# Spreading an attention tile's loads and store over its eight head units

## The chip, the cores and the metric

The kernel runs on one core of one Trainium2 chip. The metric is the device time in microseconds (us) of one execution, as the median of several runs. The trace is one profiled execution of the same program.

## The reference

Four graph layers follow each other on x (2708 nodes, 512 features) and a dense 0/1 adjacency `adj` (2708 x 2708), each wrapped as `x = layernorm(x + layer(x, adj))`. The change touches the first, an eight-head attention whose mask is the adjacency with ones on its diagonal:

```python
adj = jnp.maximum(adjacency_matrix, jnp.eye(n))
keys, queries, values = (jnp.einsum('nj,hjk->hnk', node_matrix, W) for W in (Wks, Wqs, Wvs))
atts = jnp.einsum('hqk,hmk->hqm', queries, keys) / key_dim ** 0.5
atts = atts - 1e+16 * (1.0 - adj)[None, :, :]
atts = jax.nn.softmax(atts, axis=-1)
return jnp.einsum('hqm,hmk,hko->qo', atts, values, Wo)
```

The other three layers (a matrix product with the adjacency, an edge attention, a normalised product) are not touched.

## The kernel before

All matrix work is fp16 with each operand split in a high and a low half, so a product is three matmuls; sums are fp32. `project` makes keys (`kk`) and values (`vv`), which stay in SBUF, and queries, which go to DRAM as `q_rows`. Then `attention` runs over T = 22 tiles of 128 query rows, and in each tile over H = 8 heads. One (tile, head) pair is a unit, numbered i = 8t + h. Every engine runs the same loop of steps (`all_steps`): in step h of tile t an engine works on units that lie 0 to 4 steps back, given by `on(back)` and `unit(m, u, h, back)`. Tiles are written in pairs, t = 2m + u, and tiles 3 to 20 are a hardware loop of two tiles per turn (`pairs`).

The life of a unit:

- PE (`scores`, L641) makes the scores in three pieces of keys, 1024, 768 and 916 wide, in two PSUM slots.
- DVE (`mask`, L766) adds the mask tile `adj[:, u, ...]`, which holds 0 where there is an edge and a huge negative number where there is none, and writes `sc`; then `largest` (L776) makes the row maximum.
- One step later ACT takes the exponential of the pieces (L719) and rounds piece 0 to fp16 (`part_high`, L735); POOL (`low`, L603, and the copy L615) makes the rest of the halves of pieces 0 and 1.
- In the same step SP turns pieces 0 and 1 by DMA (L578), four `dma_start_transpose` a unit: piece 0 high and low, piece 1 high and low, into `far`. Each waits for its half and, as `far` has two buffers, for PE's use of the unit two back (`far_used`). ACT in turn waits before L735 for the transposes of the unit two back (`far_ready`), since `part` has two buffers too.
- Two steps later PE turns piece 2 itself (L652); ACT and DVE split it (L746, L809).
- Three steps later PE multiplies with the values (L661): near keys (piece 2), then, after the last piece of scores of the current unit, far keys (pieces 0 and 1). Four steps later ACT copies the sum to `pv` (L726).

Work once a tile, for the tile before: DVE takes reciprocals at step 4, POOL scales (L620), PE turns `o` at step 5, PE multiplies with `wo` at step 7, DVE adds the residual input `xres` (L822) and makes the statistics (L410, L412), all on DVE in step 7 behind the masks of unit 7. POOL's `norm.finish` in step 7 (L421, L424, L433) normalises, in front of the `low` of unit 7, which is POOL's first work of the next step 0.

The next tile's mask is made ready on the way: SP loads the adjacency rows, DVE puts the ones on the diagonal (`diagonal`, L784) at step 4, POOL turns the whole row into the bias (L597) at step 5, and DVE's first mask of the next tile waits for it.

The SP queue issues everything in program order. All loads of a tile are issued at step 1, ahead of that step's transposes:

```python
if h == 1:
    loads(m, u)      # adj of tile t+1, q of tile t+1 in four DMAs, xres of tile t-1, store of tile t-2
if on(1):
    ...              # the four transposes of unit i-1
```

Of the kernel before, what the change touches and what calls it, by code (L numbers as in the profile page):

```python
# [19 lines left out]
ALU = mybir.AluOpType  # L20
# [3 lines left out]
P = 128  # L24
N = 2708
D = 512
H = 8
KD = 64
T = -(-N // P)
NP = T * P  # L30
# [17 lines left out]
BIG0 = 1e16  # L48
# [101 lines left out]
def after(m, u):  # L150

    return (m, 1) if u == 0 else (m + 1, 0)
# [221 lines left out]
def before(m, u):  # L374

    return (m, 0) if u == 1 else (m - 1, 1)


def is_tile(m, u, t):

    return isinstance(m, int) and 2 * m + u == t
# [68 lines left out]
NT = len(TURN_GROUPS)  # L450
assert len(PIECES) == 3 and PIECES[TURNED][0] % P == 0 and len(TURN_GROUPS[1]) <= GB
LN_P = math.log(P_S)


def attention(nc, layer, x_rows, out_rows, q_rows, adj_rows, kk, vv, wo, ident):
# [5 lines left out]
    with ExitStack() as ctx:  # L461
        s = Scope(nc, ctx, "att", layer)
        adj = s.sb("adj", [P, 2, NP])
        xres = s.sb("xres", [P, D])
        q = s.sb("q", [P, 2, 2, 2, J, P], F16)
        sc = s.sb("scores", [P, 2, N])
# [9 lines left out]
        norm = Norm(s, outs=1)  # L476
# [2 lines left out]
        ps_pv = s.ps("ps_pv", [P, BANK])  # L479
        ps_misc = s.ps("ps_misc", [P, BANK])  # L480

        adj_loaded = [s.sem(f"adj_loaded{u}") for u in range(2)]
        q_loaded = [s.sem(f"q_loaded{u}") for u in range(2)]
        xres_loaded = s.sem("xres_loaded")
        pad_clear, ones_ready, ln_p_ready = s.sem("pad_clear"), s.sem("ones_ready"), s.sem("ln_p_ready")
        diag_ready = s.sem("diag_ready")
        bias_ready = s.sem("bias_ready")
        slot_full = s.sem("slot_full")
        slot_free = s.sem("slot_free")
        nmax_ready = s.sem("nmax_ready")  # L490
# [49 lines left out]

        @block.sync
        def _(sp):
            def load_q(t, u):
                for e in range(2):
                    for half in range(2):
                        sp.dma_start(q[half * KD:half * KD + KD, u, e, :, :, :].rearrange("p a j r -> p (a j r)"),
                                     q_rows[bass.ds(t * P + e * KD, KD), :]).then_inc(q_loaded[u], 16)

            def loads(m, u):
                t = 2 * m + u  # L550
                if not is_tile(m, u, T) and not is_tile(m, u, T - 1):
                    m1, u1 = after(m, u)
                    if not is_tile(m, u, 0):
                        sp.wait_ge(slot_free, PER_TILE * t)
                    sp.dma_start(adj[:, u1, 0:N], adj_rows[bass.ds((t + 1) * P, P), :]) \
                        .then_inc(adj_loaded[u1], 16)
                    load_q(t + 1, u1)
                if not is_tile(m, u, 0):
                    if not is_tile(m, u, 1):
                        sp.wait_ge(misc_free, 2 * (t - 1))  # L560
                    sp.dma_start(xres[:, :], x_rows[bass.ds((t - 1) * P, P), :]).then_inc(xres_loaded, 16)
                    if not is_tile(m, u, 1):
                        norm.store(sp, out_rows, *before(*before(m, u)))

            def step(m, u, h, on):
                if h == 1:
                    loads(m, u)
                if on(1):
                    i, _t, _u, h1, same = unit(m, u, h, 1)
                    v = h1 % 2  # L570
                    for c in range(TURNED):
                        lo, width = PIECES[c]
                        k = slice(lo // P, (lo + width) // P)
                        if not early(i, 2):
                            wait_apart(sp, far_used[c], i - 1, pad_clear)
                        for a, made in enumerate((part_high[c], part_low[c])):
                            wait_apart(sp, made, i + 1, pad_clear)
                            sp.dma_start_transpose(far[a][:, v, k, :], part[a][:, v, lo:lo + width]) \  # L578
                                .then_inc(far_ready[c][v], 16)

            load_q(0, 0)
            sp.dma_start(adj[:, 0, 0:N], adj_rows[0:P, :]).then_inc(adj_loaded[0], 16)
            all_steps(sp, step)
            norm.store(sp, out_rows, T // 2 - 1, 1)
            norm.all_stored(sp)

        @block.gpsimd
        def _(pool):
            nc.gpsimd.memset(adj[:, :, N:NP], 0.0).then_inc(pad_clear, 1)
            nc.gpsimd.memset(vv[:, :, :, P:P + 1], 1.0).then_inc(ones_ready, 1)  # L590
            nc.gpsimd.memset(ln_p[:, :], -LN_P).then_inc(ln_p_ready, 1)
            norm.exponent(nc, pool)

            def bias(m, u):
                wait_apart(pool, diag_ready, 2 * m + u + 1, pad_clear)
                big = BIG0 * Q_S * Q_S
                nc.gpsimd.tensor_scalar(out=adj[:, u, 0:N], in0=adj[:, u, 0:N], scalar1=big, scalar2=-big,  # L597
                                        op0=ALU.mult, op1=ALU.add).then_inc(bias_ready, 1)

            def low(i, v, c):  # L600
                lo, width = PIECES[c]
                wait_apart(pool, part_high[c], i + 1, pad_clear)
                nc.gpsimd.tensor_tensor(out=part[1][:, v, lo:lo + width], in0=sc[:, v, lo:lo + width],  # L603
                                        in1=part[0][:, v, lo:lo + width], op=ALU.subtract).then_inc(part_low[c], 1)

            def step(m, u, h, on):
                if on(1):
                    i, _t, _u, h1, same = unit(m, u, h, 1)
                    v = h1 % 2
                    low(i, v, 0)  # L610
                    lo, width = PIECES[1]
                    if not early(i, 2):
                        wait_apart(pool, far_ready[1][v], 32 * same, pad_clear)
                    wait_apart(pool, exp_done, NC * i + 2, pad_clear)
                    nc.gpsimd.tensor_copy(part[0][:, v, lo:lo + width], sc[:, v, lo:lo + width]) \  # L615
                        .then_inc(part_high[1], 1)
                    low(i, v, 1)
                if h == 4 and not is_tile(m, u, 0):
                    pool.wait_ge(rinv_ready, 2 * m + u)
                    nc.gpsimd.tensor_tensor(out=o[:, :].rearrange("p (h k) -> p h k", h=H), in0=pv[:, 1 - u, :, 0:KD],  # L620
                                            in1=rinv[:, :, :].broadcast_to([P, H, KD]), op=ALU.mult) \
                        .then_inc(o_done, 1)
                if h == 5 and not is_tile(m, u, T - 1) and not is_tile(m, u, T):
                    bias(*after(m, u))
                if h == 7 and not is_tile(m, u, 0):
                    norm.finish(nc, pool, *before(m, u))

            bias(0, 0)
            all_steps(pool, step)

        @block.tensor
        def _(pe):
# [44 lines left out]
            def step(m, u, h, on):  # L677
                t = 2 * m + u
                i = t * H + h
                if on(0):  # L680
                    if h == 0:
                        pe.wait_ge(q_loaded[u], 64 * (m + 1))
                    scores(i, u, h, 0)
                    scores(i, u, h, 1)
                if on(2):
# [71 lines left out]
        def _(dve):  # L757
# [20 lines left out]
                                               accum_out=nmax[:, v:v + 1]).then_inc(nmax_ready, 1)  # L778

            def diagonal(m, u):  # L780
                t = 2 * m + u
                dve.wait_ge(adj_loaded[u], 16 * m + 16)
                part_of = adj[:, u, bass.ds(t * P, P)]
                nc.vector.tensor_tensor(out=part_of, in0=part_of, in1=ident[:, :], op=ALU.max).then_inc(diag_ready, 1)  # L784

            def step(m, u, h, on):
                t = 2 * m + u
                i = t * H + h
                if on(0):
                    if h == 0:  # L790
                        dve.wait_ge(bias_ready, t + 1)
                    mask(i, u, h, 0)
                if h == 4 and not is_tile(m, u, T - 1) and not is_tile(m, u, T):
                    diagonal(*after(m, u))
                if h == 4 and not is_tile(m, u, 0):
                    dve.wait_ge(pv_out, t * H)
                    if not is_tile(m, u, 1):
# [20 lines left out]
                if h == 7 and not is_tile(m, u, 0):  # L818
                    dve.wait_ge(misc_full, 2 * t)
                    dve.wait_ge(xres_loaded, 16 * t)  # L820
                    norm.free(dve, *before(m, u))
                    nc.vector.scalar_tensor_tensor(out=norm.r[:, :], in0=ps_misc[:, :], scalar=1.0 / (O_S * W_S),  # L822
                                                   in1=xres[:, :], op0=ALU.mult, op1=ALU.add).then_inc(misc_free, 1)
                    dve.wait_ge(misc_free, 2 * t)
                    norm.statistics(nc, dve, t - 1)

            rest = len(TURN_GROUPS[-1]) * P
            nc.vector.memset(ps_t[:, NT - 1, rest - P:rest], 0.0).then_inc(rest_clear, 1)
            dve.wait_ge(pad_clear, 1)
            dve.wait_ge(ln_p_ready, 1)  # L830
            diagonal(0, 0)
            all_steps(dve, step)


# [637 lines left out]
```

## Time and profile before

| what | value |
|---|---|
| median of 3 runs | 2812.24 us (2811.44 to 2812.98) |
| the profiled execution | 2815.72 us, its span 2813.9 us |
| span, PE / DVE / ACT / POOL busy | 90% / 55% / 49% / 41% |
| masks made in the attention (POOL L597) | x22, 54.1 us |
| loads `att_adj` | x22, 1354 KB each |
| loads `att_q` | x88, 128 KB each |
| DMA queue of the program (q1) | 870272 packets, 432.93 MB, 69.6% of 16 engines' span |

The attention runs from about 220 to 1520 us of the span, with its steady part, the tiles 1 to 20, from 281 to 1434. DMA share is the mean busy share of the core's 16 DMA engines; a packet's time includes what it waits for. In the timeline a row of SPq is the issue of a DMA by the SP queue: how long the issuing instruction took, not the transfer. A number in brackets at the end of a row is the idle time of the engine before it, with what ended it.

### The profile page before, as it was taken

How to read it: one execution, taken by the hardware profiler on the slowest of the kernel's cores; microseconds unless marked ns; L12 is line 12 of the kernel's file. 1: busy time of each engine (PE TensorE's matmuls, PEld its weight loads, DVE VectorE, ACT ScalarE, POOL GpSimd, SP SyncE). 2: the span in 40 equal slices, each digit the busy share in tenths (PEclk: the TensorE clock that was granted, in tenths of full speed). 3: DMA queues.
4: the chain of work that ended last, by engine and by line, in shares of the span. 5: the costliest groups of instructions: out<-in, count | busy, mean ns of one | idle time of the engine just before them, and what ended most of it. 6: DMA issues, size and time to landing. Idle time of an engine off the chain costs nothing. (4 is left out here: it accounts for less than half of the span.)

```text
span 2813.9 us, 67215 instructions
## 1 busy us (share of the span) xinstructions
PE 2536.2 (90%) x24716; PEld 1564.6 (56%) x24716; DVE 1534.5 (55%) x2860; ACT 1388.6 (49%) x1848; POOL 1163.6 (41%) x879
## 2 busy tenths in 40 slices
PE   7998898988889888898996999799999999979998
PEld 6875566656666566565663444376444444434443
DVE  3447677766777677676772222354454555633222
ACT  3337677767777677676772322223333334323221
POOL 0007687767777677776780032200111111110232
PEclk9999899988999999998998999899999999989999
DMA  3118999999999999999994356411656667742554
GB/s 124 63 57 171 179 174 174 166 174 171 160 173 166 180 173 166 166 181 169 174 157 130 117 196 206 167 48 42 161 153 168 174 178 205 187 127 80 199 196 151
DMA packets 870507, 436.18 MB, mean 155 GB/s; under 512 B 791680, under 2 KB 810112, under 8 KB 859008
## 3 DMA queue, kind: packets, MB, share of 16 engines
q1 hardware_dynamic: 870272, 432.93, 69.6%
q8 instruction: 162, 2.65, 0.4%
q14 instruction: 73, 0.60, 0.1%
HBM read 201.15 MB, written 38.44 MB: 85 GB/s over the span
## 5 line engine op out<-in xcount | busy, mean ns | idle before, releaser
L603 POOL TENSOR_TENSOR att_part_low<-att_scores,att_part_high 128x1024 f16<-128x1024 f32 x352 | 665.7, 1894 | 291.1 <-ACT att_part_high L735 265.2
L766 DVE CUSTOM_DVE_ANT_0 att_scores<-att_slots,att_adj 128x1024 f32<-128x1024 f32 x528 | 568.3, 1092 | 185.8 <-PE att_slots L641 167.1
L719 ACT ACTIVATE att_scores<-att_scores,att_nmax 128x1024 f32<-128x1024 f32 x528 | 531.2, 1037 | 65.8 <-DVE att_nmax L776 63.2
L641 PE MATMUL att_slots<-l_kk,att_q 128*128 128x512 f16 x2112 | 499.8, 376 | 46.4 <-issue 29.0
L1300 PE MATMUL a_ps<-l_y,a_adj 128*128 128x512 f16 (+1 forms) x1936 | 431.6, 382 | 9.0 <-DVE a_adj L1314 4.7
L661 PE MATMUL att_ps_pv<-l_vv,att_far_high 128*128 128x65 f16 x4928 | 270.8, 197 | 115.2 <-DMA att_far_low<-att_part_low 114.8
L661 PEld LDWEIGHTS att_ps_pv<-l_vv,att_far_high 128*128 128x128 f16 x4928 | 258.2, 101 | 159.3 <-DMA att_far_low<-att_part_low 128.6
L1300 PEld LDWEIGHTS a_ps<-l_y,a_adj 128*128 128x128 f16 (+1 forms) x1936 | 183.1, 98 | 257.5 <-issue 42.4
L641 PEld LDWEIGHTS att_slots<-l_kk,att_q 128*128 128x128 f16 x2112 | 190.9, 102 | 223.2 <-issue 77.2
L809 DVE TENSOR_TENSOR att_near_low<-att_ps_t,att_near_high 128x512 f16<-128x512 f32 x352 | 225.7, 681 | 133.5 <-ACT att_near_high L746 133.2
L1045 PE MATMUL edge_ps_o<-l_sup,edge_pt_high 128*128 128x512 f16 x968 | 288.1, 379 | 0.0
L735 ACT ACTIVATE att_part_high<-att_scores 128x1024 f16<-128x1024 f32 x176 | 186.1, 1057 | 173.8 <-DMA att_far_low<-att_part_low 168.3
L661 PE MATMUL att_ps_pv<-l_vv,att_far_low 128*128 128x65 f16 x2464 | 263.6, 199 | 0.0
L1284 ACT ACTIVATE a_adj<-l_adj 128x2816 f16<-128x2816 f32 x44 | 112.0, 2550 | 299.8 <-DMA l_adj<-in_adj_cols 278.0
L661 PEld LDWEIGHTS att_ps_pv<-l_vv,att_far_low 128*128 128x128 f16 x2464 | 235.9, 100 | 0.0
L1031 PE MATMUL edge_slots<-l_ht 128*128 128x512 f16 x1104 | 203.5, 345 | 16.4 <-DVE edge_mx L1139 14.7
L652 PE MATMUL att_ps_t<-all_ident,att_scores 128*128 128x128 f32 (+1 forms) x1408 | 201.4, 285 | 13.8 <-DVE att_near_low L809 12.7
L746 ACT ACTIVATE att_near_high<-att_ps_t 128x512 f16<-128x512 f32 x352 | 186.7, 579 | 27.1 <-PE att_ps_t L652 27.1
L986 POOL TENSOR_TENSOR edge_xb<-edge_xres,all_b_row 128x512 f32<-128x512 f32 x22 | 28.5, 1296 | 412.5 <-DVE edge_residual L1183 404.7
L652 PEld LDWEIGHTS att_ps_t<-all_ident,att_scores 128*128 128x128 f32 (+1 forms) x1408 | 156.5, 141 | 57.5 <-DVE att_near_low L809 28.3
L1045 PE MATMUL edge_ps_o<-l_sup,edge_pt_low 128*128 128x512 f16 x484 | 183.3, 379 | 0.0
L661 PE MATMUL att_ps_pv<-l_vv,att_near_high 128*128 128x65 f16 (+3 forms) x2816 | 170.3, 193 | 0.3 <-ACT att_pv L726 0.3
(149 smaller groups left out, 3842.6 us busy)
## 6 DMA issues: line engine op xcount, KB each, us to landing
l_adj<-in_adj_cols SPq DMA_DIRECT2D x44, 1408.0 KB, 6.2
att_adj<-in_adj SPq DMA_DIRECT2D x22, 1354.0 KB, 6.8
l_adj_tiles<-in_adj SPq DMA_DIRECT2D x22, 1354.0 KB, 6.0
p_x_in<-x SPq DMA_DIRECT2D x66, 256.0 KB, 2.6
att_q<-q_rows SPq DMA_DIRECT2D x88, 128.0 KB, 6.1
a_xres<-x SPq DMA_DIRECT2D x44, 256.0 KB, 2.7
scores_rows<-edge_raw SPq DMA_DIRECT2D x8, 842.0 KB, 3.5
p_x_in<-in_x SPq DMA_DIRECT2D x22, 256.0 KB, 2.7
```

What stands on the lines that cost most here:

```text
L603: nc.gpsimd.tensor_tensor(out=part[1][:, v, lo:lo + width], in0=sc[:, v, lo:lo + width], in1=part[0][:, v, lo:lo + width], op=ALU.subtract ...
L641: mm = nc.tensor.matmul(slots[:, slot, z:z + w], q[:, u, h % 2, a, h // 2, :], kk[:, h, lo + z:lo + z + w], start=a == 0, stop=a == 1)
L652: mm = nc.tensor.transpose(ps_t[0:r, g, n * P:(n + 1) * P], sc[:, v, k * P:k * P + r], ident[:, :])
L661: mm = nc.tensor.matmul(ps_pv[:, 0:cols.stop - cols.start], halves[a][0:r, v, n, :], vv[0:r, k, h, cols], start=k == TK and a + b == 0, st ...
L719: nc.scalar.activation(sc[:, v, lo:lo + width], sc[:, v, lo:lo + width], ACT.Exp, bias=nmax[:, v:v + 1]).then_inc(exp_done, 1)
L735: nc.scalar.activation(part[0][:, v, lo:lo + width], sc[:, v, lo:lo + width], ACT.Copy) \
L746: nc.scalar.activation(near[0][:, h2 % 2, n:n + len(tiles), :], ps_t[:, g, 0:w].rearrange("p (k r) -> p k r", r=P), ACT.Copy) \
L766: nc.vector.tensor_tensor_reduce(out=sc[:, v, lo:lo + width], in0=slots[:, (NC * h + c) % 2, 0:width], in1=adj[:, u, lo:lo + width], scale ...
L809: nc.vector.tensor_tensor(out=near[1][:, h2 % 2, n:n + len(tiles), :], in0=ps_t[:, g, 0:w].rearrange("p (k r) -> p k r", r=P), in1=near[0] ...
L1031: mm = nc.tensor.matmul(slots[:, slot, z:z + w], ht[a][:, j, bass.ds(t * P, P)], ht[b][:, j, lo + z:lo + z + w], start=k == 0, stop=k == l ...
L1045: mm = nc.tensor.matmul(ps_o[:, u, :], pt[a][0:r, k, :], sup[b][0:r, k, :], start=k == 0 and a + b == 0, stop=k == T - 1 and a == 1)
L1300: mm = nc.tensor.matmul(ps[:, u, :], a16[0:r, u, k, :], y[b][0:r, k, :], start=k == 0 and b == 0, stop=k == T - 1 and b == 1)
```

## The change

The mask row is loaded in four parts (`ADJ_PARTS`, 768 columns each and a last one of 404). Step h of SP issues, now behind its transposes: at h = 0 to 3 part h of the next tile's adjacency, and at h = 0 also the store of tile t-2; at h = 4 and 5 one half of the next tile's queries each (two DMAs instead of four, 256 KB each); at h = 6 `xres` of tile t-1; at h = 7 nothing. The wait for free mask buffers goes from step 1 to step 0. POOL makes the bias in four instructions, at steps 2, 3, 5 and 6, each waiting for its own load. The diagonal is put in last: DVE takes at step 7, behind the statistics, the maximum with a scaled `off_diag` tile (0 on the diagonal, the negative number elsewhere), and waits for all four biases there. The pad columns are set to the negative number instead of 0.

```diff
+ADJ_PARTS = [(c, min(6 * P, N - c)) for c in range(0, N, 6 * P)]
+BIAS_STEPS = (2, 3, 5, 6)
+BIG = BIG0 * Q_S * Q_S
...
+            def load_q(t, u, half):
+                sp.dma_start(q[half * KD:half * KD + KD, u, :, :, :, :].rearrange("p e a j r -> p e (a j r)"),
+                             q_rows[bass.ds(t * P, P), :].rearrange("(e p) n -> p e n", e=2)).then_inc(q_loaded[u], 16)
+            def load_adj(u, t, n):
+                lo, width = ADJ_PARTS[n]
+                sp.dma_start(adj[:, u, lo:lo + width], adj_rows[bass.ds(t * P, P), lo:lo + width]) \
+                    .then_inc(adj_loaded[n][u], 16)
+            def loads(m, u, h):
                 t = 2 * m + u
                 if not is_tile(m, u, T) and not is_tile(m, u, T - 1):
-                    m1, u1 = after(m, u)
-                    if not is_tile(m, u, 0):
-                        sp.wait_ge(slot_free, PER_TILE * t)
-                    sp.dma_start(adj[:, u1, 0:N], adj_rows[bass.ds((t + 1) * P, P), :]) \
-                        .then_inc(adj_loaded[u1], 16)
-                    load_q(t + 1, u1)
-                if not is_tile(m, u, 0):
+                    _m1, u1 = after(m, u)
+                    if h < len(ADJ_PARTS):
+                        if h == 0 and not is_tile(m, u, 0):
+                            sp.wait_ge(slot_free, PER_TILE * t)
+                        load_adj(u1, t + 1, h)
+                    elif h < len(ADJ_PARTS) + 2:
+                        load_q(t + 1, u1, h - len(ADJ_PARTS))
+                if h == len(ADJ_PARTS) + 2 and not is_tile(m, u, 0):
                     if not is_tile(m, u, 1):
                         sp.wait_ge(misc_free, 2 * (t - 1))
                     sp.dma_start(xres[:, :], x_rows[bass.ds((t - 1) * P, P), :]).then_inc(xres_loaded, 16)
-                    if not is_tile(m, u, 1):
-                        norm.store(sp, out_rows, *before(*before(m, u)))
+                if h == 0 and not is_tile(m, u, 0) and not is_tile(m, u, 1):
+                    norm.store(sp, out_rows, *before(*before(m, u)))
             def step(m, u, h, on):
-                if h == 1:
-                    loads(m, u)
...
+                loads(m, u, h)
...
+            def bias(m, u, n):
+                lo, width = ADJ_PARTS[n]
+                wait_apart(pool, adj_loaded[n][u], 16 * m + 16, pad_clear)
+                nc.gpsimd.tensor_scalar(out=adj[:, u, lo:lo + width], in0=adj[:, u, lo:lo + width], scalar1=BIG,
+                                        scalar2=-BIG, op0=ALU.mult, op1=ALU.add).then_inc(bias_ready, 1)
...
-                if h == 5 and not is_tile(m, u, T - 1) and not is_tile(m, u, T):
-                    bias(*after(m, u))
+                if h in BIAS_STEPS and not is_tile(m, u, T - 1) and not is_tile(m, u, T):
+                    bias(*after(m, u), BIAS_STEPS.index(h))
...
             def diagonal(m, u):
-                dve.wait_ge(adj_loaded[u], 16 * m + 16)
+                dve.wait_ge(bias_ready, len(ADJ_PARTS) * (t + 1))
                 part_of = adj[:, u, bass.ds(t * P, P)]
-                nc.vector.tensor_tensor(out=part_of, in0=part_of, in1=ident[:, :], op=ALU.max).then_inc(diag_ready, 1)
+                nc.vector.tensor_tensor(out=part_of, in0=part_of, in1=off_diag[:, :], op=ALU.max) \
+                    .then_inc(diag_ready, 1)
...
-                        dve.wait_ge(bias_ready, t + 1)
+                        dve.wait_ge(diag_ready, t + 1)
-                if h == 4 and not is_tile(m, u, T - 1) and not is_tile(m, u, T):
-                    diagonal(*after(m, u))
...
+                if h == 7 and not is_tile(m, u, T - 1) and not is_tile(m, u, T):
+                    diagonal(*after(m, u))
```

## Rows read from the trace of the kernel before

**Rows 1.** Groups by stretch: us, busy by engine, clock, DMA share, GB/s.
```profile
281.00:1434.00 1153.00, 1005.12 (x14059) 725.65 (x14058) 825.98 (x1715) 823.31 (x1138) 850.70 (x579) 0.92 0.99 171
```

**Rows 2.** The line L597: duration ns min/median/max, first and last start.
```profile
L597 POOL TENSOR_SCALAR att_adj<-att_adj x21: 2444/2457/2472, 252.8 to 1405.9; 128x2708 f32<-128x2708 f32 x21
```

**Rows 3.** The line L578 from 281 to 1434, and who waited for it.
```profile
L578 SPq DMA_TRANSPOSE att_far_high<-att_part_high x321: 1209/1231/2675, 281.7 to 1432.0; - x161
...
  ACT att_part_high L735: 164.9, 49
...
  PE att_ps_pv L661: 108.0, 41
```

**Rows 4.** Timeline of SP, start and us, about one tile's block of loads.
```profile
739.10 0.34 SPq L555 DMA_DIRECT2D att_adj<-in_adj  x1
739.63 2.73 SPq L546 DMA_DIRECT2D att_q<-q_rows  x4
742.63 0.36 SPq L561 DMA_DIRECT2D att_xres<-in_x  x1
...
744.09 1.49 SPq L578 DMA_TRANSPOSE att_far_high<-att_part_high  x1
745.69 3.90 SPq L578 DMA_TRANSPOSE att_far_low<-att_part_low  x1
749.76 1.21 SPq L578 DMA_TRANSPOSE att_far_high<-att_part_high  x1
751.06 2.00 SPq L578 DMA_TRANSPOSE att_far_low<-att_part_low  x1
753.28 1.23 SPq L578 DMA_TRANSPOSE att_far_high<-att_part_high  x1
...
758.82 1.23 SPq L578 DMA_TRANSPOSE att_far_high<-att_part_high  x1
```

**Rows 5.** The DMA queue in a stretch without loads: packets, MB, share of 16 engines.
```profile
q1 hardware_dynamic: 3670, 0.91, 85.8%
```

**Rows 6.** Timeline of SP about the last transpose of a step 6, and of a step 7.
```profile
781.92 1.88 SPq L578 DMA_TRANSPOSE att_far_low<-att_part_low  x1
...
843.99 1.86 SPq L578 DMA_TRANSPOSE att_far_low<-att_part_low  x1
849.93 1.23 SPq L578 DMA_TRANSPOSE att_far_high<-att_part_high  x1
```

**Rows 7.** Waits of SP from 281 to 1434: us in total, times, longest.
```profile
SPq L58 <- PE att_ps_pv L661: 31.6, 13, 4.6
```

**Rows 8.** Timeline of DVE in two steps 7 and the steps 0 behind them.
```profile
782.25 0.67 DVE L822 SCALAR_TENSOR_TENSOR att_residual<-att_ps_misc,att_xres 128x512 f32<-128x512 f32 x1
...
784.17 1.22 DVE L766 CUSTOM_DVE_ANT_0 att_scores<-att_slots,att_adj 128x1024 f32<-128x1024 f32 x1 [0.23 <-issue]
...
845.21 1.23 DVE L766 CUSTOM_DVE_ANT_0 att_scores<-att_slots,att_adj 128x1024 f32<-128x1024 f32 x1 [4.68 <-PE att_slots L641]
```

**Rows 9.** Timeline of POOL in the same step 7.
```profile
784.10 0.19 POOL L421 TENSOR_SCALAR att_veps<-att_mv 128x1 f32<-128x1 f32 x1 [1.21 <-DVE att_mv L412]
...
787.20 2.13 POOL L603 TENSOR_TENSOR att_part_low<-att_scores,att_part_high 128x1024 f16<-128x1024 f32 x1
```

**Rows 10.** The line L561 (`xres`) from 281 to 1434: issue to landing.
```profile
DMA to landing us min/median/max: 3.0/6.4/7.1
```

**Rows 11.** Timeline of SP in the last full tile, which loads only xres and stores.
```profile
1430.76 0.58 SPq L561 DMA_DIRECT2D att_xres<-in_x  x1
...
1431.96 1.42 SPq L578 DMA_TRANSPOSE att_far_high<-att_part_high  x1
1433.49 1.38 SPq L578 DMA_TRANSPOSE att_far_low<-att_part_low  x1
1435.05 1.59 SPq L578 DMA_TRANSPOSE att_far_high<-att_part_high  x1
```

**Rows 12.** The DMA queue from 739.9 to 749.5, and from 1431.7 to 1434.0.
```profile
q1 hardware_dynamic: 1276, 2.57, 102.4%
...
q1 hardware_dynamic: 335, 0.53, 82.6%
```

More of the change, by code:

```diff
@@ L452 @@
 LN_P = math.log(P_S)
+ADJ_PARTS = [(c, min(6 * P, N - c)) for c in range(0, N, 6 * P)]
+BIAS_STEPS = (2, 3, 5, 6)
+BIG = BIG0 * Q_S * Q_S
+assert len(ADJ_PARTS) == len(BIAS_STEPS)
 def attention(nc, layer, x_rows, out_rows, q_rows, adj_rows, kk, vv, wo, ident):
@@ L463, in attention @@
         adj = s.sb("adj", [P, 2, NP])
+        off_diag = s.sb("off_diag", [P, P])
         xres = s.sb("xres", [P, D])
@@ L480, in attention @@
         ps_misc = s.ps("ps_misc", [P, BANK])
-        adj_loaded = [s.sem(f"adj_loaded{u}") for u in range(2)]
+        adj_loaded = [[s.sem(f"adj_loaded{n}{u}") for u in range(2)] for n in range(len(ADJ_PARTS))]
         q_loaded = [s.sem(f"q_loaded{u}") for u in range(2)]
@@ L485, in attention @@
         pad_clear, ones_ready, ln_p_ready = s.sem("pad_clear"), s.sem("ones_ready"), s.sem("ln_p_ready")
+        off_diag_scaled = s.sem("off_diag_scaled")
+        bias_ready = s.sem("bias_ready")
         diag_ready = s.sem("diag_ready")
-        bias_ready = s.sem("bias_ready")
         slot_full = s.sem("slot_full")
@@ L542, in _ @@
         def _(sp):
[L543 to L549, printed above, removed]
+            def load_q(t, u, half):
[6 more added lines that the diff above has]
+            def loads(m, u, h):
                 t = 2 * m + u
                 if not is_tile(m, u, T) and not is_tile(m, u, T - 1):
-                    m1, u1 = after(m, u)
-                    if not is_tile(m, u, 0):
-                        sp.wait_ge(slot_free, PER_TILE * t)
-                    sp.dma_start(adj[:, u1, 0:N], adj_rows[bass.ds((t + 1) * P, P), :]) \
-                        .then_inc(adj_loaded[u1], 16)
-                    load_q(t + 1, u1)
-                if not is_tile(m, u, 0):
+                    _m1, u1 = after(m, u)
[6 more added lines that the diff above has]
+                if h == len(ADJ_PARTS) + 2 and not is_tile(m, u, 0):
                     if not is_tile(m, u, 1):
@@ L579, in step @@
                                 .then_inc(far_ready[c][v], 16)
-            load_q(0, 0)
-            sp.dma_start(adj[:, 0, 0:N], adj_rows[0:P, :]).then_inc(adj_loaded[0], 16)
+                loads(m, u, h)
+            for half in range(2):
+                load_q(0, 0, half)
+            for n in range(len(ADJ_PARTS)):
+                load_adj(0, 0, n)
             all_steps(sp, step)
@@ L588, in _ @@
         def _(pool):
-            nc.gpsimd.memset(adj[:, :, N:NP], 0.0).then_inc(pad_clear, 1)
+            nc.gpsimd.memset(adj[:, :, N:NP], -BIG).then_inc(pad_clear, 1)
             nc.gpsimd.memset(vv[:, :, :, P:P + 1], 1.0).then_inc(ones_ready, 1)
@@ L592, in _ @@
             norm.exponent(nc, pool)
[L594 to L598, printed above, removed]
+            nc.gpsimd.tensor_scalar(out=off_diag[:, :], in0=ident[:, :], scalar1=BIG, scalar2=-BIG, op0=ALU.mult,
+                                    op1=ALU.add).then_inc(off_diag_scaled, 1)
+            def bias(m, u, n):
[3 more added lines that the diff above has]
+                                        scalar2=-BIG, op0=ALU.mult, op1=ALU.add).then_inc(bias_ready, 1)
             def low(i, v, c):
@@ L622, in step @@
                         .then_inc(o_done, 1)
-                if h == 5 and not is_tile(m, u, T - 1) and not is_tile(m, u, T):
-                    bias(*after(m, u))
+                if h in BIAS_STEPS and not is_tile(m, u, T - 1) and not is_tile(m, u, T):
+                    bias(*after(m, u), BIAS_STEPS.index(h))
                 if h == 7 and not is_tile(m, u, 0):
                     norm.finish(nc, pool, *before(m, u))
-            bias(0, 0)
+            for n in range(len(ADJ_PARTS)):
+                bias(0, 0, n)
             all_steps(pool, step)
@@ L681, in step @@
                     if h == 0:
-                        pe.wait_ge(q_loaded[u], 64 * (m + 1))
+                        pe.wait_ge(q_loaded[u], 32 * (m + 1))
                     scores(i, u, h, 0)
@@ L830, in _ @@
             dve.wait_ge(ln_p_ready, 1)
+            dve.wait_ge(off_diag_scaled, 1)
             diagonal(0, 0)
```

## The prediction, made before the run

> **What bounds the kernel now.** I read the page first: the attention takes nearly half the span, and nothing else is touched. Its steady part shows no engine at its limit, ACT at 823 of 1153 us and PE, by a view that counts waiting matmuls, at 1005, with a clock of 0.92; what stands out is a DMA share of 0.99 [rows 1]. Next the period of a tile: the mask is made 21 times between 252.8 and 1405.9, so a tile takes 1153.1 / 20 = 57.65 us [rows 2]. Then I went by the line that issues the transposes, because ACT waited 164.9 us and PE 108.0 us for it, about 8 and 5 us a tile [rows 3].
>
> The waits alone invite the easy sum "5 us of PE a tile, given back". The timeline of SP says otherwise, and I take it as the bound. Issuing a transpose takes SP 1.21 to 1.3 us, whether the queue is empty or full and for six blocks as for eight (least 1.209, median 1.231 over 321) [rows 3, 4]. Two starts of the same transpose a unit apart, 753.28 and 758.82 with four transposes from the one to the other, make 5.54 us a unit [rows 4], so 44.3 us a tile for eight. To this comes the block of loads, 739.10 to 744.09, 5.0 us of pure issue. Behind the block the queue is full and SP's instructions are stretched: 1.49 for 1.23, 3.90 for 1.29, 2.00 for 1.24, together 3.6 us [rows 4]. SP stands still where the program jumps back for the next pair of tiles: 845.85 to 849.93, 4.1 us, for PE's far products [rows 6]; the view of waits has 31.6 us of this kind in 20 tiles [rows 7]; I take 4.1 every second tile, 2.05 a tile. 44.3 + 5.0 + 3.6 + 2.05 = 54.95; the 2.7 left of 57.65 are lone stretched transposes, such as the 1.88 at 781.92 [rows 6]. So SP's time is the tile's time. ACT and PE wait because SP is late, mostly in one piece behind the block, and a stall that moves elsewhere is worth nothing unless SP's own sum gets smaller.
>
> The 16 DMA engines come close behind: in 5.5 us without loads the queue is busy 85.8% with one unit's 3670 packets, 4.7 us a unit against SP's 5.54 [rows 5].
>
> The Trainium skill (DMA: Bandwidth & Descriptors, Issuing engines are not separate DMA queues) has the sequencer's issue time as usually small beside the DMA itself. The trace disagrees for these transposes: 5.54 us of issue against 4.7 of engines. By the page the transfers would be the bound, which is the second rival's case.
>
> **The change part by part, as SP's sum for a tile.**
>
> *Transposes.* Unchanged, 44.3.
>
> *Issue of loads.* One adjacency load with what lies behind it takes 739.63 - 739.10 = 0.53; four make 2.1. The four q DMAs take 742.63 - 739.63 = 3.0, 0.75 each; two of double size, taken at the same price, make 1.5. xres and the store take 744.09 - 742.63 = 1.46 together [rows 4]. Sum 5.1, so +0.1. Were the q DMAs priced by bytes they would be 3.0, +1.5 more; that is the upper bound.
>
> *Stretching behind loads.* The 3.6 of the block go. What the separate loads cost is not shown for adjacency pieces. The nearest row is the last full tile, which loads xres and stores, 0.53 MB, between transposes: the next three take 1.42, 1.38 and 1.59 for 1.23, 1.29 and 1.21 [rows 11], 0.7 in all. The block has 2.57 MB [rows 12], 4.8 times as much, so 3.4 us by bytes. The lower bound is zero: a unit leaves the engines 5.54 - 4.7 = 0.8 us, and the load's own issue 0.5 more. Nearer to the row, 3.0: -0.6.
>
> *Order of the SP queue.* `xres` is moved from step 1 to step 6, past five steps and their 20 transposes, and DVE wants it in step 7. Here is the change's price. In the tile shown SP ends step 6 at 781.92 + 1.88 = 783.80 [rows 6], and DVE starts L822 at 782.25 [rows 8]. A load issued then has landed, at the least seen, 3.0 us later [rows 10]; with 0.3 to issue, at about 787.1. DVE would stand 4.9 us. Behind it on DVE are the statistics, now the diagonal, and the first mask of the next tile; behind that mask PE's third piece of scores and its far products; and POOL's `finish` holds back the `low` of unit 7. What returns to SP, counted from its end of step 6 (S): xres at S + 3.3. POOL begins `finish` 1.85 after L822's start and takes 3.1 (784.10 to 787.20), then a `low` takes 2.13 [rows 8, 9]: the low half of piece 0 of unit 7 is there at S + 10.4. SP has issued xres and unit 6 by S + 6.2 and the high half of unit 7 by S + 7.5: it stands 2.9 us. By the other way, the next mask starts 1.92 after L822 (784.17 - 782.25) and 0.5 for the diagonal, at S + 5.7; behind a mask at 845.21 SP went on 4.7 later, at 849.93 [rows 6, 8], so at S + 10.4, against S + 6.2: 4.2 us. I take 3.3 in tiles without a jump. With a jump the DVE's stand lies beside PE's own, which put off the mask by 4.68 [rows 8], and I leave 4.1. Mean 3.7 for 2.05: +1.65. Lower bound +0.4 (2.9 and nothing at jumps beyond what overlaps), upper +2.7 (both ways one behind the other, 6 and 4.1 and a little).
>
> *The other moves.* The second half of q is issued a unit and a load before S, at about 783.8 - 6.2 = 777.6, and landed by 780.9; the first mask of the next tile, at 784.17 [rows 8], needs the scores made from it. That leaves PE about 3 us: hidden, by a margin that is gone if SP is later still, and then some 1 us a tile. The bias in four costs POOL perhaps 0.4 us more than one of 2.46 [rows 2]; it is hidden, since POOL's halves lie ready before SP takes them. Each part has two or three steps from load to bias. The diagonal is in the 0.5 above. The mask-buffer wait and the store's wait are met when SP comes to step 0: all masks, and `finish`, precede the transposes of unit 7. The first tile's mask may be ready a microsecond earlier.
>
> *Sum.* -0.6 + 0.1 + 1.65 = +1.15 us a tile, times 20 tiles that have both neighbours, +23 us. The profiled execution took 2815.7, so 2839 for such a one; it lay 3.5 above the median, so 2812.2 + 23 = 2835 as a median.
>
> The Trainium skill (DMA: Bandwidth & Descriptors, Bandwidth) tells to batch loads to 1 MiB and more. Between its 64 KB and its 1 MB a transfer has a fixed part of some 0.6 us (an estimate from that table); three more pieces would be 1.8 us a tile, 36 us. It speaks against the change, in the direction of the second rival.
>
> **Rivals.**
>
> *Faster.* The mechanism: pieces are swallowed by the engines' slack, and xres comes before it is missed, since SP is less far behind without the block. Stretching 0.5, stand 2.05 as before: -3.1 + 0.1 = -3.0 a tile, -60; with half of the new stand left, -2.2, -44. I put it at 2768. For it: the largest stretch of a tile, 3.9, is due to the block alone [rows 4]. Against it: SP's margin to xres is negative by 4.9 us, and the decision point is that margin: SP must end step 6 at least 3.3 us before L822. The easy sum, all of PE's 108 us given back, would be 2704; SP's sum leaves no room for it beyond 3.6 + 2.05 us a tile.
>
> *The engines become the bound.* Units 8 x 4.7 = 37.6; loads by the pair's 2.3 us for 0.53 MB (the stretch 1431.7 to 1434.0) 11.2 us for 2.57 MB, where one block had 9.6 [rows 12]; the lone stretches, no longer taken up by slack, 2.7 grown to perhaps 7.5; SP's stand 3.7, as nothing is queued then. 60.0 against 57.65, +47; with 0.3 us of restart for each of four adjacency pieces, +70: about 2875.
>
> *No change.* The saved stretch (up to 3.6) is just paid by the stand (1.65 to 2.7): within 0.2%, 2807 to 2818. It needs stretching of about 1.9 a tile.
>
> **How the numbers follow.** Slower as summed: 0.37, its own range 2819 to 2860 (stretching 2 to 3.4, stand +1 to +2.7). Engines the bound: 0.20. No change: 0.14. Faster: 0.29, of which a tenth at the easy sum. The likeliest is 2835. To hold 8 in 10 I go down to 2758, through the faster case, and up to 2890, through the engines' case. A measurement of this kernel tells about 0.2% from no change, 5.6 us. Faster 0.29, same 0.14, slower 0.57.
>
> **What the profile would show.** Right: L822 waits for a DMA of xres, 3 to 5 us in most tiles; the 7 us waits of ACT before L735 are gone, yet the period read from the masks is 58 to 59.5; transposes of 3.5 us and more are gone, but those of 1.4 to 2.0 are more; in the tiles without a jump SP stands 3 to 4 us once, for `far_used` or `part_low`. Engines the bound: transposes at 1.8 and more behind each load. Wrong: L822 without a wait means that SP is less late than I read; a period of 55 or less means that stretching was the whole of it; PE waits for q at step 0, a cost that I put at nothing.

## The result, and the profile after

The change makes the kernel slower: 2865.03 us (2862.76 to 2867.21) against 2811.84, a ratio of 1.0193, interval 1.0175 to 1.0211. The forecast was slower, by 23 us; it is 53. The time lies inside the stated range of 2758 to 2890 and the direction was right, but the forecast slowdown is less than half of the measured one, and 2865 also lies above the 2819 to 2860 that the prediction gave to its own mechanism.

The line where the residual input is added, which was L822 and is L839 now (durations least/median/most, first and last start; then what ended its engine's idle time):

```profile
L839 DVE SCALAR_TENSOR_TENSOR att_residual<-att_ps_misc,att_xres x20: 690/692/693, 322.8 to 1468.7; 128x512 f32<-128x512 f32 x20
its engine sat idle before it (us, times) until:
  DMA att_xres<-in_x: 110.1, 19
```

DVE waits for `xres` in every tile, 110.1 us over 19, or 5.8 each; before there was no wait at all. The 20 starts give the period: (1468.7 - 322.8) / 19 = 60.3 us, against 57.65 read in [rows 2]. Some 2.6 us a tile times 20 are the 53 us; there is nothing to look for outside the attention's steady part.

The same stretch as [rows 1]:

```profile
281.00:1475.00 1194.00, 990.83 (x13891) 719.05 (x13890) 847.37 (x1696) 811.37 (x1126) 854.73 (x634) 0.93 0.97 164
```

DMA share is 0.97 for 0.99, the clock 0.93 for 0.92: neither the DMA engines nor TensorE's granted clock got worse. The waits name what did. The columns are us in total, times, longest, from 281 to 1460. First those of the engines, then, from the view of SP's own waits, what answers to [rows 7]:

```profile
ACT att_part_high L752 <- DMA att_far_low<-att_part_low: 144.1, 96, 3.1
...
PE att_slots L658 <- DVE att_mx L783: 103.1, 20, 6.9
...
PE att_ps_pv L678 <- DMA att_far_low<-att_part_low: 55.1, 48, 2.3
...
DVE att_scores L783 <- issue: 28.4, 8, 3.9
```
```profile
SPq L58 <- PE att_ps_pv L678: 91.3, 19, 6.8
```

Spreading did what it does at first sight: PE's waits for transposes fell from 108.0 us to 55.1, none longer than 2.3. A new wait took their place, PE for DVE's mask, 103.1 us in 20 pieces, one a tile. SP, the engine that sets the period, stands (waits with nothing to issue) for 91.3 us until PE is done, instead of 31.6 [rows 7]: 3.0 us a tile more.

A jump is the place where the program goes back for the next pair of tiles, once every second tile. The timeline of DVE and of SP, and one row of POOL, show the stand in a tile without a jump, where SP ends step 6 at 921.36 + 1.24 = 922.60:

```profile
925.91 0.69 DVE L839 SCALAR_TENSOR_TENSOR att_residual<-att_ps_misc,att_xres 128x512 f32<-128x512 f32 x1 [5.61 <-DMA att_xres<-in_x]
...
927.69 0.29 DVE L802 TENSOR_TENSOR att_adj<-att_adj,att_off_diag 128x128 f32 x1
928.33 1.23 DVE L783 CUSTOM_DVE_ANT_0 att_scores<-att_slots,att_adj 128x1024 f32<-128x1024 f32 x1 [0.35 <-DVE att_adj L802]
```
```profile
921.36 1.24 SPq L589 DMA_TRANSPOSE att_far_low<-att_part_low  x1
922.87 0.35 SPq L574 DMA_DIRECT2D att_xres<-in_x  x1
...
927.56 1.24 SPq L589 DMA_TRANSPOSE att_far_low<-att_part_low  x1
932.84 1.23 SPq L589 DMA_TRANSPOSE att_far_high<-att_part_high  x1
```
```profile
930.95 2.13 POOL L619 TENSOR_TENSOR att_part_low<-att_scores,att_part_high 128x1024 f16<-128x1024 f32 x1
```

With S = 922.60, xres is there at S + 3.3, the mask starts at S + 5.7, and SP, done with unit 6 at S + 6.2, goes on at S + 10.2: it stands 4.0 us. POOL's low half is ready at 933.08, S + 10.5, and would alone have cost 3.0. In a tile with a jump of the program it is longer:

```profile
864.38 0.69 DVE L839 SCALAR_TENSOR_TENSOR att_residual<-att_ps_misc,att_xres 128x512 f32<-128x512 f32 x1 [4.50 <-DMA att_xres<-in_x]
...
866.14 0.29 DVE L802 TENSOR_TENSOR att_adj<-att_adj,att_off_diag 128x128 f32 x1
870.27 1.23 DVE L783 CUSTOM_DVE_ANT_0 att_scores<-att_slots,att_adj 128x1024 f32<-128x1024 f32 x1 [3.84 <-issue]
```
```profile
866.90 1.24 SPq L589 DMA_TRANSPOSE att_far_low<-att_part_low  x1
874.79 1.23 SPq L589 DMA_TRANSPOSE att_far_high<-att_part_high  x1
```

Here 3.84 us lie between DVE's diagonal and its mask, and no semaphore ended them ("issue"). They are DVE's own jump to the next turn of the loop, one every second tile. In [rows 8] the mask at 845.21 waited 4.68 us for PE, and DVE's jump lay inside that: before the change only 0.9 us of DVE's idle time at the mask was put down to "issue", now 28.4 us in 8 pieces. DVE comes to its jump 5 us late, so the jump comes behind the stand. SP stands 874.79 - 868.14 = 6.65 us here. Over the 20 tiles of the table further down it stands 7.0 us on average at the 8 jumps and 4.0 in the other 12.

### The profile page after: what moved, and what is told of

The parts are those of the page before. It is cut to its first block and busy times, and to the rows that moved or that the text cites. A ratio compares the mean times of both kernels' runs of the same rounds, so it can differ in the third digit from the quotient of the medians.

```text
span 2864.1 us, 67407 instructions
## 1 busy us (share of the span) xinstructions
PE 2530.9 (88%) x24716; PEld 1565.0 (55%) x24716; DVE 1565.9 (55%) x2860; ACT 1385.4 (48%) x1848; POOL 1178.7 (41%) x946
## 5 line engine op out<-in xcount | busy, mean ns | idle before, releaser
L669 PE MATMUL att_ps_t<-all_ident,att_scores 128*128 128x128 f32 (+1 forms) x1408 | 198.1, 282 | 10.2 <-DVE att_near_low L826 9.8
```

The source lines that it names most:

```text
L669: mm = nc.tensor.transpose(ps_t[0:r, g, n * P:(n + 1) * P], sc[:, v, k * P:k * P + r], ident[:, :])
```

## The experiments

Two theories. A: the order of SP's queue; xres, moved behind step 6, makes DVE stand, and the stand comes back to SP. B: the spreading itself; separate transfers cost issue and engine time, and the stand is harmless because SP is behind anyway. Every ratio is against runs of the kernel before on the same chip, whose median was 2812 to 2814. The edits are shown shortened; what is left out only carries the shown change through.

**xres back in step 1.**

```diff
-                if h == len(ADJ_PARTS) + 2 and not is_tile(m, u, 0):
+                if h == 1 and not is_tile(m, u, 0):
```

> The changed kernel with one edit: xres is issued in step 1 instead of step 6. Theory A (order of the queue): the slowdown is DVE's stand of 5 to 7 us at L839, which costs SP 3.0 us a tile; without it the 3.0 us come back, 20 x 3.0 = 60 us, so 2800 to 2812, L839 without a wait, SP standing only at the jumps. Rival B (the spreading itself: separate transfers take more engine and issue time, and the stand costs nothing because SP is behind anyway): 2845 or more.

Measured 2793.05, ratio 0.9934 (0.9922 to 0.9946): 72 us below the changed kernel. L839 has no wait, and SP's waits for PE are down to this:

```profile
SPq L58 <- PE att_ps_pv L678: 9.9, 8, 4.5
```

A holds. The time is 7 us below the expected 2800 to 2812, and the price of the order 12 us more than the expected 60: SP also stands less than before the change (9.9 us for 31.6), an effect that was not priced. The rest of the change is a gain of 19 us. TensorE's granted clock is 0.97 here for 0.93 in the changed kernel, so part of the 72 us could be the clock; that was not separated. The slowdown itself can't be: there the clock was 0.93 for 0.92.

**xres in step 5** (the same line, `h == 5`).

> The changed kernel with xres issued in step 5, behind the second half of q. A unit of SP lies between steps 5 and 6, some 5.8 us, and the stand at L839 is 4.5 to 6.8. Theory A: the stand shrinks to 0 to 1 us, the time falls nearly as far as with step 1, to 2803 to 2820. Rival B: 2845 or more.

Measured 2793.42, ratio 0.9931 (0.9917 to 0.9946). L839 waits 13.6 us in 10 tiles, the longest under 2. The time is below the expected 2803 to 2820 and as good as with step 1. One unit of SP's queue earlier is enough: the cost is a matter of a margin.

**The block of before, xres alone in step 6.**

```diff
+                if h == 6 and not is_tile(m, u, 0):
+                    late_xres(m, u)      # behind the transposes; no longer in loads()
```

> The kernel before with one edit: xres alone goes to step 6, behind its transposes; the other loads stay in one block at step 1. Theory A: the stand appears here too, 4 to 6 us a tile, and costs 3.0 us a tile: 2812 + 60 = about 2870 (2850 to 2885). Rival B: no more than 2825.

Measured 2868.62, ratio 1.0191 (1.0171 to 1.0211). The one edit makes a slowdown as large as the whole change's: DVE waits 86.6 us for xres in 19 tiles, and SP stands 4.5 us a tile for 2.0 while its other times stay as they were (table below). B is out.

**The queries in two DMAs, all else as before.**

```diff
-                for e in range(2):
-                    for half in range(2):
+                for half in range(2):      # each with both e, as in the change
```

> The kernel before with the queries loaded by two DMAs instead of four. If SP's issue time counts even inside the block, 1.2 us a tile is saved: 2812 - 24 = 2788. If the block's own transfers (9.6 us against 5.0 us of issue) set the time there, the saved issue turns into longer stretching and nothing changes: 2807 to 2817. I expect the second.

Measured 2819.93, ratio 1.003 (1.0018 to 1.0043): no gain, rather 8 us lost, a little above the expected 2807 to 2817. In the profiled execution, at 2814 the fastest of the ten, issue and the time between issues fell by 0.9 us a tile (9.1 to 8.2) and stretching grew by 1.2 (6.7 to 7.9): the issue saved inside the block came back as stretching. Where the 8 us of the median lie is not to be seen there.

**Spread, xres in step 1, the adjacency whole in step 0.**

```diff
-                lo, width = ADJ_PARTS[n]
-                sp.dma_start(adj[:, u, lo:lo + width], adj_rows[bass.ds(t * P, P), lo:lo + width]) \
+                if n == 0:
+                    sp.dma_start(adj[:, u, 0:N], adj_rows[bass.ds(t * P, P), :])...
```

> The kernel of the run with xres in step 1, with the adjacency loaded whole in step 0 (the bias stays in four, all waiting for the one load). If the four parts are what lowers the stretching, the block's long stretched transpose comes back and the time goes up to 2800 to 2812. If only q, xres and the store had to leave the block, it stays at 2785 to 2797, since three issues of about 0.5 us a tile are saved as well.

Measured 2798.08, ratio 0.9952 (0.9933 to 0.997), against 0.9934 (0.9922 to 0.9946) with four parts. It lies between the two expectations, and the intervals overlap: whether the four parts pay was not told apart. The profiles show why the difference is small: loaded whole, the adjacency saves 1.9 us of issue and time between issues a tile (8.2 for 10.0) and costs 2.2 of stretching (8.0 for 5.8).

**The loop of four tiles in the changed kernel.**

```diff
-            pairs(eng, 3, T - 1, tile)
+            with eng.Fori(0, 4) as i:
+                for t in range(3, 7):
+                    tile(i * 2 + t // 2, t % 2)
+            tile(9, 1)
+            tile(10, 0)
```

> The changed kernel with a hardware loop of four tiles per turn (tiles 3 to 18, then 19 and 20 written out): 4 or 5 jumps in place of 9. If DVE's own jump comes behind its stand (3.8 us in series, SP standing 6.8 us instead of 4.0), a jump costs 2.8 us: about 14 us less, 2851. If the jump lay beside the stand, as the prediction took it, no change: 2860 to 2870.

Measured 2852.15, ratio 1.0137 (1.0116 to 1.0159), 13 us less than the changed kernel, and 2851 was expected. That is the size which a jump in series gives: DVE's "issue" pieces at the mask are 3 instead of 8, and five jumps at 2.6 us (6.65 - 4.04) are 13.

**The same loop with xres in step 1.**

> The kernel with xres in step 1, with the same loop of four tiles. Without the stand DVE's jump lies beside PE's, and SP stands only 0.85 us a tile in all, so a saved jump is worth 1 us or so: 2785 to 2793.

Measured 2787.09, ratio 0.9919 (0.9901 to 0.9938), as expected, and not told apart from 0.9934. By the medians the four-tile loop gives 13 us where DVE stands and 6 where it does not, by the tile periods of the profiled executions 12 and 3; only the first is clear of noise.

**Bias in four and diagonal last, all loads in one block at step 1,** the adjacency whole and the queries in two DMAs.

```diff
+                if h == 1:
+                    for part_n in (1, 2, 3, 0, 4, 5, 6):
+                        loads(m, u, part_n)
...
-                loads(m, u, h)
```

> The changed kernel with all its loads and the store back in one block at step 1, ahead of the transposes, the adjacency whole and the queries in two DMAs: what is left of the change is the bias in four parts and the diagonal put in last. To be held against the kernel before with the queries in two DMAs, 2820. If this part costs nothing, as predicted for the bias and the diagonal without a stand: 2814 to 2826. If the diagonal on the way to the first mask counts, 0.5 us a tile: about 2830.

Measured 2816.92, inside the expected 2814 to 2826, ratio 1.0016 (1.0004 to 1.0029), against 1.003 for the same loads without it. The intervals overlap: this half of the change costs nothing that can be measured.

**Loads and store issued by ACT.** The step's `loads` goes from the end of SP's step to the end of ACT's, xres in step 1:

```diff
-                loads(m, u, h)             # SP
+                loads(act, m, u, h)        # ACT, after the rest of its step
```

> The kernel with xres in step 1, with the loads and the store of each step issued by ACT at the end of its own step instead of by SP; SP issues transposes alone. If SP's issue time is the bound, its sum loses the loads, 6.8 us a tile with the time between them, against perhaps 2 to 3 us more stretching as the engines come nearer their limit: 4 us x 20 = 80 us less than 2793, about 2713 (2690 to 2750). If the DMA engines are the bound, they have the same packets: 2780 to 2800.

Measured 2729.92, ratio 0.97 (0.9681 to 0.972). The same packets, on the same 16 engines, cost 63 us less when SP does not issue them (80 less was expected, with 2690 to 2750 as the range). In the steady part the DMA engines now move 182 GB/s, against 175 with xres in step 1 and 171 before, so the transfers had room: SP's issue time was the bound.

**The same with the loop of four.**

> The same with the hardware loop of four tiles. With SP no longer behind, a jump of PE (3.7 us) is less hidden, so a saved jump is worth 2 to 4 us: 10 to 20 us less than the run with loads on ACT.

Measured 2721.21, ratio 0.9676 (0.9653 to 0.9698), the fastest of all by its median. It is 9 us below the run above, a little short of the expected 10 to 20, and the intervals overlap.

**Loads on ACT, xres in step 6.**

> Loads on ACT, but xres back in step 6, as in the changed kernel. What made xres late was its place behind the transposes of SP's queue, not the step by name: ACT comes to the end of step 6 some 5 us before DVE wants xres, and 3 us are enough. So within 10 us of the run with loads on ACT and xres in step 1, and L839 without a wait over 1 us. If step 6 is too late in any queue, 40 to 60 us more.

Measured 2730.43, ratio 0.9711 (0.9687 to 0.9735), with no wait at L839, both as expected. Step 6 was never too late by name; behind SP's transposes it was.

**Loads on ACT in one block at step 1.**

```diff
-                loads(act, m, u, h)
+                if h == 1:
+                    for n in range(7):
+                        loads(act, m, u, n)
```

> Loads and store issued by ACT as in the run with loads on ACT, but all of a tile in one block at the end of ACT's step 1 (the adjacency still in four parts). SP's issue sum is the same as there. If the other queue is what pays, and the spreading little, 2725 to 2745. If the spreading matters too, the block's 9 us of transfers stop the transposes once a tile and ACT's own work waits behind 4 to 5 us of issue: 2750 to 2790. I expect the second.

Measured 2863.13, ratio 1.0188 (1.015 to 1.0225), 133 us more than spread, and far beyond the expected 2725 to 2745 and 2750 to 2790. The timeline of SP behind a block shows where:

```profile
816.95 1.39 SPq L589 DMA_TRANSPOSE att_far_low<-att_part_low  x1
818.67 4.39 SPq L589 DMA_TRANSPOSE att_far_high<-att_part_high  x1
823.15 6.59 SPq L589 DMA_TRANSPOSE att_far_low<-att_part_low  x1
829.91 1.21 SPq L589 DMA_TRANSPOSE att_far_high<-att_part_high  x1
```

Two transposes take 11.0 us instead of 2.5, where the block in SP's own queue stretched its followers by 3.6 [rows 4]. ACT is held up as well while it issues the block:

```profile
ACT att_pv L742 <- issue: 76.3, 20, 4.6
```

That is 3.8 us a tile. SP's own sum grows by 5.8 us of stretching a tile against the spread loads while it stands no longer than there, and its period grows by 5.6; so the stretching is enough to explain the loss. What ACT's delay would cost by itself was not tried.

## Why the prediction was right in direction and wrong in size

SP's time by the rows of its timeline, us a tile over 20 tiles (first to 21st start of the residual line; the last of them is a short one, so the period is 59.9 here and 60.3 above). Stretching is what an issue takes above 1.25 us (a transpose) or 0.8 (a load); SP stands where more than 0.5 us lies between two issues:

| | before | changed | before, xres in step 6 | xres in step 1 | loads on ACT | loads on ACT, block |
|---|---|---|---|---|---|---|
| transposes, up to 1.25 each | 39.5 | 39.7 | 39.6 | 39.7 | 39.6 | 39.7 |
| loads, and the time between issues | 9.1 | 9.9 | 9.2 | 10.0 | 4.6 | 4.7 |
| stretching | 6.7 | 5.1 | 6.8 | 5.8 | 7.4 | 13.2 |
| SP stands | 2.0 | 5.2 | 4.5 | 0.8 | 2.4 | 2.0 |
| period | 57.3 | 59.9 | 60.1 | 56.3 | 54.0 | 59.5 |

*SP's time is the tile's time: right, and shown* by the loads on ACT.

*Issue of loads, +0.1.* It is +0.8. The prices of single issues were near enough (median 0.43 for a part of the adjacency), but a load between transposes brings more time between the issues than one in a block, which I did not price.

*Stretching, -0.6.* It is -1.6: the choice of 3.0 near the byte-scaled row was too high. That these two misses, +0.7 and -1.0 us a tile, nearly cancel is luck.

*Order of the SP queue, +1.65: the step that failed by its size.* It is +3.0 by the view of waits and +3.2 in the table, above the upper bound of +2.7 too. The mechanism, its place and its times from S were right to 0.2 us. Two sizes were not. In tiles without a jump I took 3.3 between my own two routes, 2.9 and 4.2, and the row shows 4.0, with 3.0 for the other route: the later route decides, so the choice should have been the greater of the two and nothing between them. At jumps I wrote that the DVE's stand "lies beside PE's own" and left 4.1; it is 6.65 in the tile shown and 7.0 on average. I had priced PE's jump from its row and not seen that DVE has one too, hidden under a 4.68 us wait for PE. Once the stand made DVE the last, its jump came in series; the loop of four gives 13 us back, as that price says.

*The bias and the diagonal, the waits for mask buffers and the store, q at step 0.* Hidden as said: the block with bias and diagonal is level, SP waited 0.5 us for mask buffers, once, and PE 1.2 us for q, once.

*The signs.* DVE's wait for xres came, 4.5 to 6.8 us instead of 3 to 5; ACT's waits of 7 us are gone (longest 3.1) and so are transposes above 3.5 us (longest 3.4); the period is 60.3 where 58 to 59.5 was foretold, which is the mis-sized stand again.

*The rivals.* "Faster" rested on the margin of xres: DVE stood 5.8 us (4.9 in the prediction). Had it been met, 2793 and not 2768 would have come. "The engines become the bound" gave nearly the measured time from a wrong cause: with the same transfers xres in step 1 is 72 us faster. That its number is near is luck. Its 0.3 us of restart for each piece was read from no row and no run shows it; nor do the 36 us that the prediction worked out for three more pieces appear, with 2793.05 for four parts and 2798.08 for the whole.

By the Trainium skill (DMA: Bandwidth & Descriptors, Issuing engines are not separate DMA queues) DMAs from several engines share the same 16 engines and only the sequencer's time is saved, usually little. The block from ACT agrees with the first half, for it stretches SP's transposes. The second half does not agree here, where the sequencer's time was worth 63 us.

## What to carry to other kernels

Where a queue issues everything in order, price each moved transfer by when its consumer wants it against when the queue comes to the new place, at the queue's worst lag, and not by the step's name. When two routes lead to the same wait, take the later one, and when a stall makes another engine the last, add what that engine had hidden under its old waits. If an issuing queue is the bound, try moving plain loads to another queue: here that gave more than any order tried inside it (2730 against 2793), but only with the loads spread.

## What was not expected of the hardware

A block of loads and the store, 2.4 MB, issued from ACT while SP issues transposes stretches two of these to 4.39 and 6.59 us, and 13.2 us a tile in all. The same bytes in SP's own queue leave 6.7 us of stretching a tile, 3.6 of it behind the block, and spread over steps from ACT they leave 7.4. Why two queues stretch each other so was not shown.

Each engine's jump back takes time of its own: 3.84 us on DVE in the tile shown and 3.7 us on average on PE (29.8 us over 8). PE's is seen in the kernel before too (29.0 us over 8); DVE's is hidden there (0.9 us in all) and comes to 28.4 us over 8 in the changed kernel. Five jumps fewer were worth 13 us where DVE's came behind its stand; where it did not, no gain was told from noise.
